# A recurrent block and two MLPs on one core: the first chunk's mixing products in full fp32, and its neighbours' weight splits moved later

## Reference

```python
# first sublayer, a gated linear recurrence, then a gated MLP, inside a residual and a layer norm
t  = rmsnorm(x) * norm1_w
xb = causal_conv4(t @ Wx)                       # 4 taps, per channel, + conv_b
r, i = sigmoid(xb @ Wa), sigmoid(xb @ Wi)
a  = exp(-8 * softplus(lam) * r)
h  = scan(a, sqrt(max(1 - a*a, 1e-12)) * (i * xb))   # along the sequence
h1 = x + (h * gelu(t @ Wy)) @ Wo
u  = rmsnorm(h1) * norm2_w
x  = layernorm(x + h1 + (gelu(u @ Wg) * (u @ Wu)) @ Wd)
# second sublayer
x  = layernorm(x + relu(x @ W1 + b1) @ W2 + b2)
```

## Time and profile before

| | us |
|---|---|
| median of 3 runs (lowest to highest) | 622.78 (621.52 to 623.34) |
| profiled execution | 621.15 |
| its span, first to last instruction | 619.4 |
| PE busy | 601.3 (97%) |
| DVE busy | 386.9 (62%) |
| ACT busy | 309.0 (50%) |
| POOL busy | 205.1 (33%) |

### The profile page before, as it was taken

The page is one execution under the profiler, slowest core; times in us unless marked ns, Lnnn a source line. Parts: engine busy times, 40 slices in busy tenths (PEclk is TensorE's granted clock), DMA queues, the critical chain, the costliest instruction groups (busy, mean ns, idle before and its releaser), DMA issues.

```text
span 619.4 us, 9569 instructions
## 1 busy us (share of the span) xinstructions
PE 601.3 (97%) x3681; PEld 536.6 (87%) x3681; DVE 386.9 (62%) x698; ACT 309.0 (50%) x580; POOL 205.1 (33%) x307
## 2 busy tenths in 40 slices
PE   7999988999999999999999999999999999999996
PEld 6897877789988898889888898888988898888996
DVE  5795676736585747747477465748467473663565
ACT  4865733365453754447444644537544473322353
POOL 5614137211724135130732216241451405241131
PEclk9999999999999999999999999999999999999999
DMA  8601001000100001010010101001000100000011
GB/s 274 228 2 34 1 2 35 0 1 2 34 1 1 34 1 36 2 34 1 1 35 2 34 1 35 0 1 35 2 1 1 35 1 1 1 19 18 0 35 35
DMA packets 13085, 15.69 MB, mean 25 GB/s; under 512 B 600, under 2 KB 12272, under 8 KB 13040
## 3 DMA queue, kind: packets, MB, share of 16 engines
q1 hardware_dynamic: 13040, 15.09, 7.2%
HBM read 10.89 MB, written 4.19 MB: 24 GB/s over the span
## 4 chain that ended last, share of the span: by engine, by line
PE 86%; DVE 8%; ACT 2%; POOL 2%; issue 1%; DMA 1%; POOLq 0%; DVEq 0%
PE psum L313 17%; PE psum L315 17%; PE psum L314 17%; PE psum L321 10%; PE psum L323 10%; PE psum L322 10%; PE psum L328 3%; DVE xb L847 1%; POOL normed L1218 1%; DVE row L922 1%; DVE xv L883 1%; DMA xs<-in_L_attn_x_dram 1%; PE psum L445 1%; PE psum L443 1%; PE psum L441 1%
## 5 line engine op out<-in xcount | busy, mean ns | idle before, releaser
L1247 POOL TENSOR_SCALAR gu_hi<-gu_raw 128x512 fp32r<-128x512 f32 x64 | 50.8, 794 | 318.3 <-DVE gu_raw L945 318.3
L955 DVE TENSOR_TENSOR hid_lo<-hid_raw,hid_hi 128x512 fp32r<-128x512 f32 x56 | 45.5, 813 | 83.9 <-ACT hid_hi L703 83.9
L699 ACT ACTIVATE hid_raw<-psum,vecs 128x512 f32<-128x512 f32 x56 | 38.4, 686 | 114.0 <-PE psum L315 114.0
L945 DVE TENSOR_TENSOR gu_raw<-psum,gu_raw 128x512 f32<-128x512 f32 x64 | 44.1, 689 | 81.3 <-PE psum L315 78.9
L321 PE MATMUL psum<-w_d_hi,gu_hi 128*128 128x256 f32 x256 | 72.8, 285 | 2.4 <-DVE gu_lo L950 2.4
L321 PE MATMUL psum<-w_hi,hid_hi 128*128 128x256 f32 x256 | 71.7, 280 | 0.6 <-DVE hid_lo L960 0.4
L323 PE MATMUL psum<-w_hi,hid_lo 128*128 128x256 f32 x256 | 71.8, 281 | 0.0
L323 PE MATMUL psum<-w_d_hi,gu_lo 128*128 128x256 f32 x256 | 71.8, 280 | 0.0
L322 PE MATMUL psum<-w_lo,hid_hi 128*128 128x256 f32 x256 | 71.7, 280 | 0.0
L322 PE MATMUL psum<-w_d_lo,gu_hi 128*128 128x256 f32 x256 | 71.6, 280 | 0.0
L690 ACT ACTIVATE gu_raw<-psum 128x512 f32<-128x512 f32 x64 | 38.1, 596 | 49.1 <-PE psum L315 48.4
(11 more groups left out here) (166 smaller groups left out, 1574.4 us busy)
## 6 DMA issues: line engine op xcount, KB each, us to landing
xs<-in_L_attn_x_dram SPq DMA_DIRECT2D x8, 512.0 KB, 3.5
out_dram<-row SPq DMA_DIRECT2D x15, 256.0 KB, 2.2
raw<-in_L_ffn_W_dram SPq DMA_DIRECT2D x2, 1024.0 KB, 13.0
raw_gud<-in_L_attn_Wg_dram SPq DMA_DIRECT2D x1, 1024.0 KB, 8.4
raw_gud<-in_L_attn_Wu_dram SPq DMA_DIRECT2D x1, 1024.0 KB, 10.5
raw_gud<-in_L_attn_Wd_dram SPq DMA_DIRECT2D x1, 1024.0 KB, 12.7
raw_xyai<-in_L_attn_Wx_dram SPq DMA_DIRECT2D x1, 256.0 KB, 2.8
raw_xyai<-in_L_attn_Wy_dram SPq DMA_DIRECT2D x1, 256.0 KB, 3.0
```

The source lines that it names most:

```text
L699: nc.scalar.activation(hid_raw[:, w % SLOTS, :], bank[:, :], ACT.Relu, bias=vec("b1", m)).then_inc(relu_ready, 1)
L945: nc.vector.tensor_tensor(gu_raw[:, r % SLOTS, :], up_bank(r)[:, :], gu_raw[:, r % SLOTS, :], ALU.mult).then_inc(gu_ready, 1)
L955: nc.vector.tensor_tensor(hid_lo[:, w % SLOTS, :], hid_raw[:, w % SLOTS, :], hid_hi[:, w % SLOTS, :].bitcast(FP32), ALU.subtract).then_inc ...
L1247: nc.gpsimd.tensor_scalar(gu_hi[:, r % SLOTS, :], gu_raw[:, r % SLOTS, :], 1.0, 0.0, ALU.mult, ALU.add).then_inc(gu_hi_ready, 1)
```

## The change

1. **Products.** For chunk 0 the products with Wx, Wa, Wi, Wy and Wo, and for chunk 1 those with Wx and Wy, are one fp32 matmul per block and k, straight from the raw weights and unsplit activations (`raw_step`, `raw_product`, `first_x`, `first_decay`, `first_out`). norm1_w is multiplied into the transposed tile (`first_tT`).
2. **Norms by pairs.** x of chunk 0 comes in two DMAs, and its squares, rms, normalised tiles and transposes go by pairs of token tiles; so do the norm, transposes and splits of u for chunks 0 and 1. DVE normalises x of chunk 0 and ACT u of chunks 0 and 1 (both were POOL's), DVE squares the decay of chunk 0 (was ACT's). The convolution of chunk 0 runs half by half.
3. **Splits moved.** The splits of Wa, Wi, Wx, Wy and Wo go from the ramp to rounds 0 to 4 (hi all on ACT), those of W1 and W2 from rounds 1 to 6 to rounds 8 and 9. ACT splits hi of Wg and Wu (was POOL).
4. **Loads moved.** W2 is loaded once Wd is split, W1 after x of chunk 2 and the splits of Wx, Wy, Wa, Wi, into shared space.
5. **Mixing of chunk 1 moved.** `mix_decay(1)` and `mix_input(1)` go from the ramp to round 3, two convolution steps to rounds 0 and 1, its recurrence from rounds 0 to 4 to rounds 3 to 6, `mix_out(1)` from round 5 to 6. `down(7)` goes ahead of `gate_up(8)`. `add_x_h1(0)` goes to round 2.
6. **Fillers** of the ramp: 8, 14, 5, 9, 28, 24 become 8, 1, (2, 3), 7, 4, (3, 5).

The core of the diff:

```diff
             load_x(1)
-            for n in ("g", "u", "o", "d", "1"):
+            for n in ("y", "g", "u", "o", "d"):
                 load_w(n)
             sync.dma_start(b2_rows[:, :], b2.partition_broadcast(P)).then_inc(b2_loaded, DMA)
+            sync.wait_ge(hi_split["d"], pieces["d"])
+            sync.wait_ge(lo_split["d"], pieces["d"])
             load_w("2")
             for c in range(2, CHUNKS):
                 sync.wait_ge(xh_ready, 2 * (c - 2) + 2)
                 load_x(c)
+                if c == 2:
+                    sync.wait_ge(wy_done, 2 * KD)
+                    for n in ("x", "y", "a", "i"):
+                        sync.wait_ge(hi_split[n], pieces[n])
+                        sync.wait_ge(lo_split[n], pieces[n])
+                    load_w("1")
                 if c >= 4:
...
+            def raw_step(dst, n, m, k, moving):
+                return nc.tensor.matmul(dst, raw_weight(n)[:, k, m * P:(m + 1) * P], moving[:, k, :], start=(k == 0),
+                                        stop=(k == KD - 1))
+            def raw_product(bank, n, moving, done):
+                for m in range(KD):
+                    for k in range(KD):
+                        last = raw_step(psum[bank + m][:, :], n, m, k, moving)
+                    last.then_inc(done, 1)
+            def first_x(c):
+                pe.wait_ge(first_tT_ready, 4 + 2 * c)
+                raw_product(MIX, "x", first_tT[c], wx_done)
+            def first_decay(bank):
+                for k in range(KD):
+                    pe.wait_ge(taps_added, taps_done(0, LOOKBACK - 1, k))
+                    for m in range(KD):
+                        last = raw_step(psum[bank + m][:, :], "a", m, k, xb)
+                        if k == KD - 1:
+                            last.then_inc(wa_done, 1)
+            def first_out(bank):
+                for q in range(PAIRS):
+                    for k in range(KD):
+                        if q == 0:
+                            pe.wait_ge(hy_ready, k + 1)
+                        for tt in (2 * q, 2 * q + 1):
+                            last = nc.tensor.matmul(half_bank(bank, tt), gy[:, k, toks(tt)], raw_weight("o")[:, k, :],
+                                                    start=k == 0 and tt % 2 == 0, stop=k == KD - 1,
+                                                    skip_group_check=True)
+                    last.then_inc(wo_done, 1)
...
                 mixing = n < CHUNKS
+                if r == KH:
+                    down(r - 1)
                 if units(r):
                     gate_up(r)
+                if r == 3:
+                    split_done("a", "i")
+                    mix_decay(1)
+                    mix_input(1)
                 if mixing and m == 0 and p >= 1:
                     transpose_t(n)
                 if mixing and m == 3 and p >= 1:
                     mix_decay(n)
-                if mixing and m == 7:
+                if mixing and m == 7 and p >= 1:
                     transpose_u(n)
                 if r == 1:
                     split_done("d")
-                if units(r - 1):
+                if units(r - 1) and r != KH:
                     down(r - 1)
+                if r == 6:
+                    split_done("o")
+                    mix_out(1)
+                if r == 7:
+                    transposed_by_pairs(normed, 1, u_ready, uT_done, MIX, (0, 0))
                 if mixing and m == 3 and p >= 1:
                     mix_input(n)
+                if r == KH:
+                    split_done("x")
+                if r == KH + 4:
+                    split_done("y")
                 if r == LAG_UP:
-                    split_done("1", "2")
+                    split_done("1")
+                if r == LAG_DOWN:
+                    split_done("2")
                 if units(r - LAG_UP):
...
-            mix_x(0)
-            split_done("y")
-            mix_y(0, bank=DOWN)
-            transpose_t(1)
-            keep_running(9, SECOND)
-            split_done("a", "i")
+            nc.tensor.transpose(psum[UP][:, 0:NV], vec_rows[:, :], ident[0:NV, 0:NV]).then_inc(vecs_transposed, 1)
+            keep_running(1, SECOND)
+            transposed_by_pairs(normed, 0, t_ready, tT_done, MIX, (2, 3))
+            pe.wait_ge(w_loaded["x"], DMA)
+            first_x(0)
+            keep_running(7, SECOND)
             pe.wait_ge(vecs_ready, 1)
-            mix_decay(0, bank=GATE)
-            mix_input(0, bank=SECOND)
-            mix_x(1)
+            pe.wait_ge(w_loaded["a"], DMA)
+            first_decay(GATE)
+            pe.wait_ge(w_loaded["i"], DMA)
+            raw_product(SECOND, "i", xb, wi_done)
+            pe.wait_ge(tap_done, 2)
+            pe.wait_ge(t_ready, 8)
+            transposed(normed, tT_done)
+            pe.wait_ge(w_loaded["y"], DMA)
+            raw_product(DOWN, "y", first_tT[0], wy_done)
+            first_x(1)
+            pe.wait_ge(tanh_a_ready, KD)
+            keep_running(4, GATE)
+            pe.wait_ge(w_loaded["o"], DMA)
+            pe.wait_ge(tanh_i_ready, KD)
+            first_out(SECOND)
             pe.wait_ge(gy_ready, KD)
-            mix_y(1, bank=DOWN)
-            pe.wait_ge(tanh_a_ready, KD)
-            keep_running(28, GATE)
-            split_done("o")
-            mix_out(0, bank=GATE)
-            pe.wait_ge(tanh_i_ready, KD)
-            keep_running(24, SECOND)
-            transpose_u(0)
-            mix_decay(1, bank=SECOND)
-            pe.wait_ge(gy_ready, 2 * KD)
-            mix_input(1, bank=DOWN)
-            split_done("g", "u")
+            raw_product(DOWN, "y", first_tT[1], wy_done)
+            transposed_by_pairs(normed, 0, u_ready, uT_done, GATE, (3, 5))
             for r in range(UNITS):
...
+                if mixing and m == 6 and p >= 1:
                     square_h1(n)
                 if units(r):
                     gelu_gate(r)
                 if mixing and p == 0:
                     if m == 0:
+                        weight_hi("a")
+                        weight_hi("i")
+                    if m == 1:
+                        xb_hi(n)
+                    if m == 2:
+                        weight_hi("x", "n1")
+                        weight_hi("y", "n1")
+                    if m == 3:
+                        tanh_decay(n)
                         exp_decay(n)
+                        tanh_input(n)
                         square_decay(n)
                         act.preload_act_table(ACT.Gelu_apprx_tanh)
-                    if m == 2:
+                    if m == 4:
                         gate_scale(n)
                         act.preload_act_table(ACT.Gelu_apprx_tanh)
-                    if m == 1:
-                        weight_hi("1")
-                    if m == 3:
-                        weight_hi("2")
-                    if m == 4:
+                        weight_hi("o")
+                    if m == 6:
                         hy_hi(n)
+                        square_first_h1(n)
+                    if m == 7:
+                        first_norm_u(n)
+                        split_hi_by_pairs(uT_hi, n, MIX, uT_done, uT_hi_ready)
                 if mixing and p >= 1:
...
+                if r == KH:
+                    weight_hi("1")
+                if r == KH + 1:
+                    weight_hi("2")
                 if mixing:
...
-            square_x(1)
+            act.wait_ge(tT_done, 1)
+            for f in range(KD):
+                nc.scalar.activation(first_tT[0][:, f, half(0)], pair_bank(MIX, 0)[:, f, :], ACT.Copy,
+                                     scale=vec("n1", f)).then_inc(first_tT_ready, 1)
             conv_start(0, 0)
             conv_start(0, 1)
-            gelu_y(0, bank=DOWN)
-            xb_hi(0)
-            split_hi(tT_hi, tT_done, tT_hi_ready, 1)
+            square_x(1)
+            weight_hi("g", "n2", ks=[0])
             tanh_decay(0, bank=GATE)
-            weight_hi("o")
             act.wait_ge(consts_ready, 1)
             exp_decay(0)
-            square_decay(0)
             tanh_input(0, bank=SECOND)
             gate_scale(0)
             act.preload_act_table(ACT.Gelu_apprx_tanh)
-            hy_hi(0)
+            gelu_y(0, bank=DOWN)
+            weight_hi("g", "n2", ks=[1])
+            weight_hi("u", "n2", ks=[0])
             conv_start(1, 0)
             conv_start(1, 1)
+            square_first_h1(0)
+            weight_hi("u", "n2", ks=[1])
+            first_norm_u(0)
+            split_hi_by_pairs(uT_hi, 0, GATE, uT_done, uT_hi_ready)
             gelu_y(1, bank=DOWN)
...
+            def first_norm_t():
+                for q in range(PAIRS):
+                    dve.wait_ge(rms1_rstd, q + 1)
+                    for tt in (2 * q, 2 * q + 1):
+                        nc.vector.tensor_scalar(normed[:, tt, :], xs[0][:, tt, :], rstd1[:, tt:tt + 1], None,
+                                                ALU.mult).then_inc(t_ready, 1)
+            def squared_decay():
```

(92 more changed lines are left out.)

245 lines of the change are left out of this document (141 added, 104 removed).

## The result

| | before | after |
|---|---|---|
| median of 20 runs (lowest to highest), us | 622.75 (621.52 to 624.51) | 624.24 (622.74 to 625.66) |
| profiled execution, us | 621.15 | 624.24 |
| its span, us | 619.4 | 622.5 |
| mean granted clock in it | 0.998 | 0.987 |

The ratio is 1.0026, with a 95% interval of 1.0017 to 1.0035: 0.3% slower. The forecast was 623.5 and +0.7 us; the medians are 1.5 us apart, the two profiled executions 3.1 us.

A forecast was written before the change was run, and what follows sets the result against it. PE was taken as fed without a gap from the first `mlp_up`, which waits for busy DVE. Ramp -13.5, period 0 +7.8, period 1 +4.5, clock +1.9 give +0.7: 623.5 us from 622.78, range 618.0 to 626.5.

The forecast's parts named there:

- the ramp: Start of kernel up to S, the first `gate_up`: S falls from 56.49 to 43.0 us, a gain of 13.5.
- period 0: From S, first `gate_up`, to T, first `gate_up` of period 1: grows from 41.1 to 48.9 us, +7.8.
- the start of period 1: From T, its first `gate_up`, to M, first `mlp_up`: W1 and W2 splits on DVE add 4.5 us, 18.9 to 23.4.
- the clock behind M: After M, the first `mlp_up`: PE's 5.7 us wait before it drops the clock to 1.2 GHz, costing 1.9 us.
- The fp32 price: Raw products in the ramp: an fp32 matmul of 512 columns takes 0.91 us on PE, at least 0.85.
- the last step: End of ramp: DVE's Wg and Wu splits; it loses a POOL piece, 1.05 us, so first `gate_up` is 43.0, not 42.0.
- in round 3 the split of Wa and Wi is ready as PE arrives: Period 0, round 3: PE has no wait for this split, arriving 14.5 us after the first `gate_up`.
- The argument that waits of 2.2 us do not make the clock fall: Waits of 2.2 us in round 7 of the old kernel left the clock up; 5.7 us will drop it.
- 1, that the clock does not fall: Rival on PE's wait before the first `mlp_up`: clock stays full, 621.6 us; chance 0.14.
- 4, that the splits hide: Rival on rounds 8 and 9: W1 and W2 splits cost nothing, no clock fall, 617.1 us; chance 0.10.
- 2, a shorter ramp and period 0: Rival: both come out 3 us shorter (POOL's piece, fp32 price, Wo wait), 620.5 us, 618.6 without clock fall; chance 0.20.
- 3, the late mixing chain: Rival in rounds 3 to 6: chunk 1's mixing is late, 0.7 us per place missed, 626.3 with four; chance 0.22.

The follow-up runs named there:

- Run 8: Changed kernel with DVE's split of Wg moved ahead of the first h1 addition and fillers (2, 3) for (3, 5): 622.73 us, ratio 0.9999 to before.
- Run 3: Changed kernel with 20 filler matmuls in PE's wait of round 10, ahead of the first `mlp_up`: 621.70 us, ratio 0.9994 to before.
- Run 4: Changed kernel with POOL's `add_x_h1(0)` in round 3 instead of round 2: 622.43 us, ratio 0.9992 to before.
- run 1: Kernel before with only the splits of W1 and W2 moved to rounds 8 and 9, W2 loaded after Wd's split: 627.52 us, ratio 1.0078 to before.
- run 2: Changed kernel with the splits of W2 put into round 3 and of W1 into rounds 6 and 7: 619.17 us, ratio 0.9945 to before.
- run 6: Changed kernel with `down(7)` back behind `gate_up(8)` and the transposes of chunk 2: 623.81 us, ratio 1.0022 to before.

## Why the prediction was right, and where it was not

**The forecast held** (+0.7 forecast, +1.5 measured), and for its main reason: the ramp's gain is eaten in period 0 and at the start of period 1. That it is so close is in part luck. The profiled execution, +3.1, misses it by 2.4: the ramp gave 0.7 more, T to M 0.3 and the clock behind M 0.2, while period 0 took 3.7 more, of which 1.4 are falls of the clock that not every execution need have at both places. The medians hide 1.6 us of this miss, because before was profiled in one of its fastest executions, 1.6 us under its median, and after in one at its median.

**The ramp: right in size** (42.28 for 43.0). The fp32 price is right: 8 recorded pieces, four matmuls, take 3.67 us, 0.92 each for 0.91. `first_x(0)` starts 0.75 later than worked out, `first_out` at 31.26 for 31.45. Wrong is the last step. I had POOL's w_d_hi lock out DVE's Wu piece, for 1.05 us. It is the other way round: DVE's split of Wg locks out POOL's rms. That rms ends at 39.2 instead of 38.2, w_d_hi starts behind it, and DVE, its Wu piece done in 1.28, waits 0.82 for ACT. Run 8 shows it: without Wg's split there the power takes 0.70, and S comes 0.97 earlier. So the term of 1.05 had about the right size, but for a reason that the rows don't bear out.

**Period 0: too short by 3.7 us.** Run 3 has no fall of the clock there and shows PE's waits bare:

| PE waits in period 0 | predicted | run 3 | after |
|---|---|---|---|
| `down(0)` | 0.6 | 0.36 | 0.39 |
| split of Wa and Wi | 0 | 2.04 | 2.01 |
| `down(5)` | 2.5 | 2.50 | 2.21 |
| `mix_out(1)` | 1.9 | 1.54 | 0.29 |
| round 7 | 0.9 | 0.45 | 0.45 |
| S to T | 48.9 | 51.19 | 52.57 |

From S to T run 3 has 51.19 us, 44.16 busy and 7.03 idle; before had 41.11, 36.36 busy and 4.75 idle. So 7.8 us of work came in and 2.3 us of waits. The prediction had 6.8 of work and waits "as many as now", having taken now's for 5.8. Its sum doesn't come out either: 41.1 with 5.4 and 1.4 added is 47.9, and its own items (35.2 of old work, 6.8 of new, 6 of stalls) give 48.0, where 48.9 stands. The 0.9 too much happened to cover a part of PE's work, which was priced 2.2 too low (42.0 for 44.16). So the 3.7 us are 1.3 of work, 1.0 of waits and 1.4 that goes with the clock.

The step that failed is "in round 3 the split of Wa and Wi is ready as PE arrives": PE waited 2.04 us there. The other waits were 1.05 shorter in all than forecast. The walk had `add_x_h1(0)` in the diff, and priced it at nothing; it reads SBUF on POOL for 2.98 us, and DVE's split stood still beside it. Run 4 removes it, and S to T is 49.06. Against run 3, after has 1.4 more (52.57 less 51.19), which goes with the clock at half rate behind two waits: PE is busy for 2.9 us more and idle for 1.5 less, as slower matmuls arrive later at the wait for hy, which shrinks from 1.54 to 0.29. The argument that waits of 2.2 us do not make the clock fall, as in round 7 of before, was a reading of a single execution.

**Start of period 1: right** (23.12 for 23.4), with the right mechanism, shown by both signs: the moved splits alone bring it into the old kernel (run 1), and taking them away brings 18.83 back (run 2). The 0.71 us that DVE waits for ACT's hi of x1T, predicted as 0.6, is in the timeline, and of DVE's old idle time 0.83 hid the pieces, predicted as 0.9.

**The clock in round 10: right** (1.65 for 1.9), shown by run 3. **`down(7)` worth nothing: right**, run 6.

**The rivals.** 1, that the clock does not fall, is out: the windows of after show the fall, and run 3, which has none in round 10, is 2.0 us faster. 4, that the splits hide, is out by run 1. 2, a shorter ramp and period 0, had one part of three: S was 0.7 early, the Wo wait stayed. 3, the late mixing chain, did not happen as told: `down(5)` and `mix_out(1)` waited 4.04 in run 3 where 4.4 were forecast. The us that were missing were lost one step earlier, on the weights' own split.

**What stays open.** The 20 executions of after have mean clocks of 0.987 to 0.995, all below the 0.999 of run 3's profiled execution and the 0.998 of before's, so each had some more time at half rate; where, only the profiled one shows. Before has such executions too: in the 23 that ran beside runs 1 to 4, those up to 621.71 us have a mean clock of 0.997 to 1.000, those of 622.59 and more 0.992 to 0.997. No profile here caught one, so where before loses them isn't known, nor how much of the difference between the two kernels is a difference in how often the clock falls.
